# Feed-forward product from split operands: the low parts are formed in the bank by the tensor engine

## What is computed

```python
x = layernorm(x + mixer(x))
h = einsum('bsd,nrd->nbsr', x, lora_A)
coef = (2.0 * lora_weights)[:, None, None]
lora_out = einsum('nbsr,nor->bso', h, lora_B * coef)
base = einsum('bsd,od->bso', x, W) + bias
x = layernorm(x + base + lora_out)
```

## Time and profile before

| | |
|---|---|
| median of 3 runs | 1603.32 us (1602.87 to 1603.79) |
| the profiled execution | 1602.69 us, its span 1600.8 us |
| PE busy | 1579.3 us, 99% of the span |
| DVE busy | 1350.8 us, 84% |
| POOL busy | 1229.3 us, 77% |
| ACT busy | 1223.6 us, 76% |
| mean granted clock of PE | 0.999 of full speed |
| PE's share of the chain that ended last | 95% |

### The profile page before, as it was taken

One profiled execution on the slowest core, in us unless ns is written; L12 is line 12 of the kernel. 1 busy time (PEld: TensorE's weight loads), 2 busy tenths in 40 slices (PEclk: granted clock), 3 DMA queues, 4 the chain that ended last, 5 costly groups with the idle time before them and its releaser, 6 DMA issues.

```text
span 1600.8 us, 27372 instructions
## 1 busy us (share of the span) xinstructions
PE 1579.3 (99%) x9112; PEld 1300.4 (81%) x9112; DVE 1350.8 (84%) x1878; ACT 1223.6 (76%) x2367; POOL 1229.3 (77%) x1019
## 2 busy tenths in 40 slices
PE   8999999999999999999999999999999999999998
PEld 6778888888888888888888888888888888888765
DVE  6776898879979798787988879887998879888797
ACT  5888778886778877887877877888777886778743
POOL 4578788787796868778787887878688786887874
PEclk9999999999999999999999999999999999999999
DMA  3732324233242433433243332433324333343311
GB/s 116 251 129 90 123 81 158 82 116 107 90 143 94 123 99 100 129 100 119 81 123 128 99 122 74 146 102 108 115 87 139 103 116 105 101 129 99 124 55 60
DMA packets 87148, 178.69 MB, mean 112 GB/s; under 512 B 16480, under 2 KB 20576, under 8 KB 86624
## 3 DMA queue, kind: packets, MB, share of 16 engines
q1 hardware_dynamic: 86000, 176.77, 34.1%
q10 hardware_dynamic: 1008, 0.17, 0.1%
HBM read 172.17 MB, written 4.72 MB: 111 GB/s over the span
## 4 chain that ended last, share of the span: by engine, by line
PE 95%; POOL 1%; DVE 1%; issue 1%; DMA 1%; ACT 1%; ACTq 0%; POOLq 0%; SPq 0%; DVEq 0%
PE proj L513 16%; PE proj L514 16%; PE proj L515 16%; PE p_yd L689 8%; PE p_out L561 7%; PE p_out L563 7%; PE p_out L562 7%; PE p_st L570 5%; PE p_hid L525 4%; PE proj L625 2%; PE p_st L699 1%; PE p_st L701 1%; PE p_st L700 1%; PE p_misc L536 1%; DMA raw<-w_t 0%
## 5 line engine op out<-in xcount | busy, mean ns | idle before, releaser
L513 PE MATMUL proj<-x_hi,w_hi 128*128 128x512 f32 x1160 | 461.8, 398 | 8.2 <-DVE x_lo L1300 6.9
L514 PE MATMUL proj<-x_lo,w_hi 128*128 128x512 f32 x1160 | 452.9, 390 | 0.0
L515 PE MATMUL proj<-x_hi,w_lo 128*128 128x512 f32 x1160 | 452.9, 390 | 0.0
L1018 POOL TENSOR_TENSOR w_lo<-raw,w_hi 128x512 fp32r<-128x512 f32 x209 | 284.2, 1364 | 103.7 <-ACT w_hi L751 100.8
L1175 DVE SCALAR_TENSOR_TENSOR hs<-proj,uch,hs 128x511 f32<-128x511 f32 (+2 forms) x384 | 285.6, 744 | 42.8 <-ACT hs L778 38.0
L832 ACT ACTIVATE decay<-decay,tok 128x128 f32<-128x128 f32 x1024 | 312.4, 391 | 0.0
L513 PEld LDWEIGHTS proj<-x_hi,w_hi 128*128 128x128 f32 x1160 | 218.8, 189 | 54.1 <-issue 12.0
L515 PEld LDWEIGHTS proj<-x_hi,w_lo 128*128 128x128 f32 x1160 | 218.3, 188 | 45.9
L514 PEld LDWEIGHTS proj<-x_lo,w_hi 128*128 128x128 f32 x1160 | 218.9, 189 | 42.2
L1204 DVE TENSOR_TENSOR decay<-decay,cb 128x1024 f32<-128x1024 f32 x128 | 200.0, 1563 | 54.7 <-ACT decay L850 53.0
L1076 POOL TENSOR_TENSOR dh<-dh,eac 128x512 f32<-128x512 f32 x96 | 127.2, 1325 | 144.5 <-DVE eac L1235 144.5
(11 more groups left out here) (138 smaller groups left out, 3029.1 us busy)
## 6 DMA issues: line engine op xcount, KB each, us to landing
decay<-acum_d SPq DMA_DIRECT2D x128, 512.0 KB, 4.4
raw<-w_t SPq DMA_DIRECT2D x209, 256.0 KB, 3.0
eac<-eacum_d SPq DMA_DIRECT2D x192, 128.0 KB, 3.0
wo_raw<-wo_t SPq DMA_DIRECT2D x32, 256.0 KB, 4.0
c_new<-wo_t SPq DMA_DIRECT2D x32, 256.0 KB, 4.3
hs<-x_t SPq DMA_DIRECT2D x8, 256.0 KB, 5.6
acc<-x_tok SPq DMA_DIRECT2D x1, 2048.0 KB, 8.2
out<-acc SPq DMA_DIRECT2D x8, 256.0 KB, 2.0
```

The costliest lines, as they stand in the source:

```text
L513: nc.tensor.matmul(dst[:], w_hi[:, ws, k, :], x_hi[:, k, cols], start=(k == 0), stop=False)
L514: nc.tensor.matmul(dst[:], w_hi[:, ws, k, :], x_lo[:, k, cols], start=False, stop=False)
L515: mm = nc.tensor.matmul(dst[:], w_lo[:, ws, k, :], x_hi[:, k, cols], start=False, stop=(k == KC - 1))
L1018: nc.gpsimd.tensor_tensor(w_lo[:, s].rearrange("p a b -> p (a b)"), raw[:, s, :], w_hi[:, s].rearrange("p a b -> p (a b)").bitcast(F32), A ...
```

## The change

The weight and the turned tile are split into high and low fp32r parts, and the product of a tile becomes twelve fp32r products instead of four fp32 ones. The low part is made in the bank: ACT copies the bank rounded into the high part, PE adds minus that high part through a negative identity (fold_rest for the weight, the first product of ffn for the tile), and ACT copies what is left as the low part. PE also adds the weight itself to the low-rank product by an identity in fp32, and DVE's fold_weight goes. The split weight lies in x_hi and x_lo, the split tile in w_hi and w_lo, which the mixer no longer needs then. The negative identity is written by ACT into x_hi.

In order: fold_rest(0) ends step 2 on PE; fold_rest(1) and turn(0) stand in step 3 before and after project_out(2), fold_rest(2) ends it; fold_rest(3) and project_out(3) stand ahead of ffn(0) in step 4. ACT's folded_lo(1) opens step 3 and folded_lo(3) step 4, ahead of gaps and exponentials; turned_lo(c - 4) stands behind them. In the tail ffn(4) comes ahead of turn(5), ffn(5) and ffn(6) have a turn between their high and their low products, and the last tile is done whole. DVE adds it and takes its statistics whole.

```diff
+        yT_hi, yT_lo = lambda t: w_hi[:, t % 2], lambda t: w_lo[:, t % 2]
+        ffn_w_hi, ffn_w_lo = lambda k: x_hi[:, k, 0:HID], lambda k: x_lo[:, k, 0:HID]
+        minus_ident = x_hi[:, 0, HID:HID + P]
...
                 wait(pe, w_folded, k - 1)
                 nc.tensor.matmul(FFN_BANK(k), lora_a_sb[:, k * P:(k + 1) * P], lora_b_sb, start=True, stop=False)
+                nc.tensor.matmul(FFN_BANK(k), ident[:], ffn_w_sb[:, k, :], start=False, stop=False)
...
+            def fold_rest(k):
+
+                pe.wait_ge(fold_hi_ready, k + 1)
+                nc.tensor.matmul(FFN_BANK(k), minus_ident, ffn_w_hi(k), start=False, stop=True,
+                                 skip_group_check=True).then_inc(fold_rest_ready, 1)
...
             def ffn(t, between=None):
 
+                pe.wait_ge(yt_hi_ready, t + 1)
+                nc.tensor.matmul(proj[0][:], minus_ident, yT_hi(t).rearrange("p k l -> p (k l)"), start=False, stop=True,
+                                 skip_group_check=True).then_inc(yt_rest_ready, 1)
                 pe.wait_ge(w_folded, KC)
                 wait(pe, ffn_sum, t - 1)
-                pe.wait_ge(yt_copied, t + 1)
                 for k in range(KC):
-                    if k == 2 and between is not None:
-                        turn(between)
-                    mm = nc.tensor.matmul(FFN_BANK(t), yT(t)[:, k, :], ffn_w_sb[:, k, :], start=(k == 0), stop=(k == KC - 1))
+                    nc.tensor.matmul(FFN_BANK(t), yT_hi(t)[:, k, :], ffn_w_hi(k), start=(k == 0), stop=False)
+                    nc.tensor.matmul(FFN_BANK(t), yT_hi(t)[:, k, :], ffn_w_lo(k), start=False, stop=False)
+                if between is not None:
+                    turn(between)
+                pe.wait_ge(yt_lo_ready, t + 1)
+                for k in range(KC):
+                    mm = nc.tensor.matmul(FFN_BANK(t), yT_lo(t)[:, k, :], ffn_w_hi(k), start=False, stop=(k == KC - 1))
                 mm.then_inc(ffn_out, 1)
...
+                        if ffn_step and c in (3, 4):
+                            fold_rest(2 * c - 5)
+                        if ffn_step and c == 4:
+                            project_out(g, e, 3)
                         if ffn_step and c >= 4:
                             ffn(c - 4)
                         if ffn_step and c in (4, 5, 6):
                             carried_out(g, e, c + 1)
-                        if ffn_step and c >= 3:
+                        if ffn_step and c >= 4:
                             turn(c - 3)
...
                             fold_lora(0)
                             fold_lora(1)
+                            fold_rest(0)
                         if ffn_step and c == 3:
+                            turn(0)
                             fold_lora(2)
                             fold_lora(3)
+                            fold_rest(2)
 
             groups(body)
+            ffn(4)
             turn(5)
-            ffn(4)
             project_out(G, 1, 7)
             norm_sum(G, 7, True)
-            turn(6)
-            ffn(5)
+            ffn(5, between=6)
             ffn(6, between=7)
-            last_ffn()
+            ffn(7)
...
+            def turned_hi(t):
+
                 act.wait_ge(ln_turned, t + 1)
                 wait(act, ffn_out, t - 1)
-                nc.scalar.activation(yT(t), proj[0][:].rearrange("p (k l) -> p k l", k=KC),
-                                     ACT.Copy).then_inc(yt_copied, 1)
+                nc.scalar.activation(yT_hi(t), proj[0][:].rearrange("p (k l) -> p k l", k=KC), ACT.Copy).then_inc(yt_hi_ready, 1)
+
+            def turned_lo(t):
+
+                act.wait_ge(yt_rest_ready, t + 1)
+                nc.scalar.activation(yT_lo(t), proj[0][:].rearrange("p (k l) -> p k l", k=KC), ACT.Copy).then_inc(yt_lo_ready, 1)
...
+                        if last and e == 1 and c in (3, 4):
+                            folded_lo(2 * c - 5)
                         o2, e2, c2 = ahead(e, c, 2)
...
+                        if last and e == 1 and c >= 4:
+                            turned_lo(c - 4)
                         late = c == 1 or (last and e == 1)
                         act.wait_ge(gated, s + 1)
...
                         if last and e == 1 and c >= 3:
-                            copy_turned(c - 3)
+                            turned_hi(c - 3)
...
+                            if c in (2, 3):
+                                folded_hi(2 * c - 4)
+                                folded_hi(2 * c - 3)
+                                folded_lo(2 * c - 4)
...
+                            nc.scalar.activation(minus_ident, ident[:], ACT.Copy, scale=-1.0).then_inc(coef_ready, 1)
 
             groups(body)
-            copy_turned(5)
+            turned_lo(4)
+            turned_hi(5)
             centre(6)
+            turned_lo(5)
             normalize(3)
-            copy_turned(6)
+            turned_hi(6)
+            centre(7)
+            turned_lo(6)
             normalize(4)
-            centre(7)
-            copy_turned(7)
+            turned_hi(7)
+            turned_lo(7)
             normalize(5)
             normalize(6)
...
-            def fold_weight(k):
-
-                dve.wait_ge(lora_ready, k + 1)
-                nc.vector.tensor_tensor(ffn_w_sb[:, k, :], ffn_w_sb[:, k, :], FFN_BANK(k), ALU.add).then_inc(w_folded, 1)
...
-            for t in range(5, CHUNKS - 1):
+            for t in range(5, CHUNKS):
                 add_ffn(t)
                 ln_begin(1, t)
```

More of the change, by code:

```diff
@@ L200, in mixer_ffn_kernel @@
         ffn_loaded, coef_ready, stored = sem("ffn_loaded"), sem("coef_ready"), sem("stored")
-        lora_ready, w_folded = sem("lora_ready"), sem("w_folded")
-        ln_turned, yt_copied, ffn_out, ffn_sum = sem("ln_turned"), sem("yt_copied"), sem("ffn_out"), sem("ffn_sum")
+        lora_ready, fold_hi_ready, fold_rest_ready, w_folded = (
+            sem("lora_ready"), sem("fold_hi_ready"), sem("fold_rest_ready"), sem("w_folded"))
+        ln_turned, yt_hi_ready, yt_rest_ready, yt_lo_ready, ffn_out, ffn_sum = (
+            sem("ln_turned"), sem("yt_hi_ready"), sem("yt_rest_ready"), sem("yt_lo_ready"), sem("ffn_out"), sem("ffn_sum"))
         sc = [hs[:, 1, k, :] for k in range(UT)] + [half[:, 2 * k:2 * k + 2, :].rearrange("p a b -> p (a b)") for k in range(4)]
@@ L609, in turn @@
             def turn(t):
                 pe.wait_ge(centred, t + 1)
-                wait(pe, yt_copied, t)
+                wait(pe, yt_lo_ready, t)
                 for k in range(KC):
-                    mm = nc.tensor.transpose(proj[0][:, k * P:(k + 1) * P], acc[:, t, k * P:(k + 1) * P], ident[:])
+                    mm = nc.tensor.matmul(proj[0][:, k * P:(k + 1) * P], acc[:, t, k * P:(k + 1) * P], ident[:], start=(k == 0), stop=(k == KC - 1),
+                                          is_transpose=True)
@@ L626, in ffn @@
-                mm.then_inc(ffn_out, 1)
[L630 to L638, removed]
+                    nc.tensor.matmul(FFN_BANK(t), yT_hi(t)[:, k, :], ffn_w_hi(k), start=(k == 0), stop=False)
@@ L714, in body @@
                                 carried_out(g, e, 2)
-                        if c:
+                        if ffn_step and c == 4:
+                            pass
+                        elif c:
                             project_out(g, e, c - 1)
@@ L818, in normalize, with folded_hi, folded_lo @@
                                      bias=shift[:, t:t + 1]).then_inc(normed, 1)
-            def copy_turned(t):
+            def turned_hi(t):
                 act.wait_ge(ln_turned, t + 1)
                 wait(act, ffn_out, t - 1)
-                nc.scalar.activation(yT(t), proj[0][:].rearrange("p (k l) -> p k l", k=KC),
-                                     ACT.Copy).then_inc(yt_copied, 1)
+                nc.scalar.activation(yT_hi(t), proj[0][:].rearrange("p (k l) -> p k l", k=KC), ACT.Copy).then_inc(yt_hi_ready, 1)
+            def turned_lo(t):
+                act.wait_ge(yt_rest_ready, t + 1)
+                nc.scalar.activation(yT_lo(t), proj[0][:].rearrange("p (k l) -> p k l", k=KC), ACT.Copy).then_inc(yt_lo_ready, 1)
+            def folded_hi(k):
+                act.wait_ge(lora_ready, k + 1)
+                nc.scalar.activation(ffn_w_hi(k), FFN_BANK(k), ACT.Copy).then_inc(fold_hi_ready, 1)
+            def folded_lo(k):
+                act.wait_ge(fold_rest_ready, k + 1)
+                nc.scalar.activation(ffn_w_lo(k), FFN_BANK(k), ACT.Copy).then_inc(w_folded, 1)
             def gaps(g, e, c):
@@ L1433, in body @@
                             scale_off(g, e, c + 1)
-                        if ffn_step and c == 3:
-                            fold_weight(2)
-                            fold_weight(3)
                         if ffn_step:
                             low_gated(s)
-                        if ffn_step and c == 2:
-                            fold_weight(0)
-                            fold_weight(1)
             groups(body)
```

17 lines of the change are left out of this document (1 added, 16 removed).

## The result

The changed kernel takes 1606.13 us (median of 21 runs, 1603.43 to 1608.19) where the kernel before takes 1603.43 us beside it (1602.20 to 1604.82). The ratio is 1.0016, 95% interval 1.0011 to 1.0022, which is 2.7 us slower (1.8 to 3.5). That is within the 0.2% (3.2 us) that I called "the same", though the interval reaches just over it. It is on the side of the forecast, 1.1 us more than the +1.6 us that I had added up: 1606.13 us where I had 1604.9.

The account below looks back on a forecast made before the run. PE and DVE were near their limit, with ACT and POOL releasing them. Product's end 0.0, unsplit tail 0.5 and one clock fall 1.1 sum to +1.6 us: 1604.9 us beside the median, range 1600.0 to 1608.0.

Parts of the forecast that it names:

- the fall at 1538: PE's clock at half speed in ffn(0) of the kernel before, a loss of 1.97 us, should go with the pauses filled.
- The pause in ffn(0): PE, done with its high products at 1543.0, waits 0.8 us for ACT's turned_lo(0).
- that in ffn(2): In step 6 PE waits about 3.6 us for ACT's turned_lo(2), with a fall of the clock expected behind it.
- case 1: The forecast: DVE and ACT set the pace and the clock falls once, 1604.9 us; chance 0.40.
- case 2: DVE and ACT set the pace without a fall of the clock, 1603.8 us; chance 0.22.
- case 5: The clock falls after each of PE's new pauses; two falls at full price, +4.4 us, 1607.7 us; chance 0.20.
- Case 4: PE alone sets the pace and the copies slip in unseen, -5.1 us, 1598.2 us; chance 0.13.
- the size of the fall: Behind PE's pause in ffn(2), carried_out(7) delayed by up to 1.97 us, of which 1.1 us reach y(7).
- The pause of 1.5 us that I predicted in ffn(4): PE, through its high products at 1579.6, waits 1.5 us for turned_lo(4), which stands behind normalize(2) on ACT.
- step 4: ACT's folded_lo(3) waits for fold_rest(3), delaying exponentials; DVE's scaling of eac comes 1.7 us late, y(5) 0.9 us.
- the unsplit tail: The last addition and its statistics, no longer split in halves, cost 0.5 us more on the last chain.
- PE prices: On PE, a token tile's feed-forward product takes 2.96 us for 3.43, gaining 0.47; the last tile gains nothing.

Follow-up runs that it names:

- three_blocks: The kernel before with the fold on PE and ACT, product unsplit, and the fourth feed-forward block of tiles 0 to 3 left out: 1601.71 us, ratio 0.9989.
- hi_thrice: The changed kernel with the eight high products of tile 2 made three times, each time afresh: 1605.48 us, ratio 1.0013.
- three_moves: The changed kernel with ACT's folded_lo(3) put between two exponentials, turned_lo(2) at the head of step 6, turned_lo(4) ahead of centre(5): 1602.63 us, ratio 0.9993.
- carried_ahead: three_moves with carried_out(5) placed between project_out(3) and ffn(0) on PE: 1600.84 us, ratio 0.9984.
- lora_twice: The kernel before with the low-rank product of each of the four blocks made twice, DVE adding as before: 1603.40 us, ratio 1.0001.
- fold_only_ffn4: The kernel before with the fold on PE and ACT, product unsplit, and ffn(4) ahead of turn(5) in the tail: 1600.64 us, ratio 0.9984.
- tail_halves: The changed kernel with the last tile's product, addition and statistics in two halves again: 1606.01 us, ratio 1.0016.
- fold3_later: The changed kernel with ACT's folded_lo(3) between two exponentials instead of ahead of the gaps: 1605.54 us, ratio 1.0010.
- lo2_ahead: The changed kernel with ACT's turned_lo(2) opening step 6, ahead of gaps and exponential of chunk 7: 1604.51 us, ratio 1.0008.

## Why the prediction was right, and where it was off

All times here are in the frame of before (after less 2.10 us).

**Right.** The fp32r products follow each other in 0.22 to 0.23 us (1551.20 and 1551.42). PE's pauses up to 1540 are filled and the fall at 1538 is gone. mix(5) starts at 1542.4 (predicted 1542.3), eac(5) at 1546.0 (1545.9), y(5) at 1550.6 (1550.4). The pause in ffn(0) is 0.78 us (0.8), that in ffn(2) 3.55 (3.6), turned_lo(2) starts at 1564.0 and ends 0.58 later, at 1564.6 (1564.4). One fall of the clock follows. So it is case 1: case 2 (no fall) is against the mean clocks of all runs, and case 5 (falls behind the other pauses too) against the trace, in which the clock stays full behind the 0.78 us, though the one fall lasts as long as the two of case 5 would. Case 4, that PE alone sets the pace, falls with three_blocks: in steps 5 and 6 it does not.

**Off: the size of the fall, and half a microsecond without it.** I let 1.1 us of the fall reach y(7), by DVE's slack, and from there the end. y(7) is at 1574.56, where I had 1573.1 + 1.1 = 1574.2, a little more. But the fall lasted 6.8 us, twice the one that I had priced. (That price, 1.97 us, was itself a little high: it compares a record, 5.40 us, with a distance of starts, 3.43; carried_out(5) starts at 1543.06, 5.23 us behind the start of the product, so the loss was 1.80.) The longer fall cost PE 2.9 us: 1.87 for the four low products that take 0.91 at full clock, and 6.43 us from carried_out(7) to the product into p_yd (1568.60 to 1575.03), where the kernel before takes 4.53:

```profile
1563.40 1.05 PE L570 MATMUL p_st<-cT,state 128*128 128x128 f32 x8
...
1567.93 1.09 PE L689 MATMUL p_yd<-decay,xdt 128*64 128x128 f32 x16
...
1592.01 1.89 PE L637 MATMUL proj<-hs,raw 128*128 128x256 f32 x8
```

PE, which I held to be ahead, was thereby the path itself: it was busy for 32.20 of the 32.20 us from 1566.80 to 1599.00. The pause of 1.5 us that I predicted in ffn(4) shrank to 0.14, because PE came late itself. The last tile starts 2.5 us later than before (1594.49 for 1592.01), where my terms give 1592.6 + 1.1, 1.7 us later. 0.8 us are missing.

hi_thrice divides them. It has the same waits and no fall, and it starts the last tile at 1593.02 (1595.81 less its own offset of 2.79 us; its y(2) is at 1521.36). So the fall is worth 1.47 us there, 0.4 more than my 1.1. The other 0.4 have nothing to do with the clock: without a fall I had 1592.6. Of them 0.27 stand in turned_lo(4), which lets PE go on at 1581.42 where I had 1581.15, and the rest in the work behind it. The mechanism was right; the term for the fall should have been 1.5, and the product's end without a fall was not level with the kernel before but 0.4 us behind it.

**Right in the sum, off in the reason: step 4.** I named ACT's folded_lo(3) as the new wait. It costs 1.0 us. Once it is out of the way, PE's own order costs more: carried_out(5) stands behind both project_out(3) and ffn(0), and with ffn(0) moved behind it 1.74 us come back between three_moves and carried_ahead. That project_out(3) alone, moved back, would give the same was not run. My arithmetic had it in it (it counted the 2.8 us of project_out ahead of ffn(0)), so that eac(5) came out right, but I did not see it as a cause of its own that the moved step puts on DVE.

**Right in the net: the last tile.** +0.5 for the unsplit tail and -0.5 for the shorter product were both in the sum, though my passage on PE prices says that the last tile gains nothing. It does: from its first product to DVE's last addition it takes 3.21 us for 3.66, and from there to the end 5.60 us for 5.13. From the first product of the tile to the last power it is 5.24 us in both kernels.

**Where the gain went.** The fold part alone gives about 2 us. The split product with its order costs 4.5 to 5 on top. By the distances from y(2) to the end, after and carried_ahead differ by 5.63 us: 1.04 is the place of folded_lo(3), 1.74 that of carried_out(5), 1.27 in y(5) to y(7) the place of turned_lo(2) with the fall behind it, and 1.5 that of turned_lo(4). Each of these is a difference of two single profiles; of the runs, the intervals of neighbouring steps overlap, and only the sum is clear of noise. What the split product saves on PE, 0.47 us a tile, comes to nothing in steps 5 and 6: y(5) to y(7) is 22.65 to 22.97 us in all kernels without a fall there, except lora_twice with 23.15. Only behind y(7), where PE sets the end, may it show: 26.9 us with the split product, 27.5 with fold_only_ffn4, two kernels that differ in more than the product. And it is lost again ahead of y(5) (29.26 for 28.80), so that the two are level from y(2) to the end, 79.10 and 78.99 us.

## What to carry to other kernels

A step moved ahead on one engine delays everything that stood between its old and its new place; ask of each instruction there who waits for it. Where two or three engines are near their limit, a cheaper product on one of them is worth nothing until its copies on the others stand where nobody waits for them; here the places decided 5.6 us, and even with all of them well placed the split product was only level with the unsplit one. Price a possible fall of the clock on the engine's own path and as if it may last twice as long as the one you have seen.

## What the runs showed of the hardware that I had not expected

- After much the same pause of PE (2.3 to 2.6 us, near 80 us) the clock fell in twelve profiles and not in two, and a fall was 3.4 or 6.8 us long, with nothing in the kernel to tell them apart. Behind the pause of 3.55 us it fell in the profiles of after and tail_halves for 6.8 us and in that of fold3_later for 3.4. Behind single pauses of 0.98, 1.41 and 1.65 us (lo2_ahead) it stayed full. What decides isn't settled.
- In the runs of the changed kernel the time goes with the mean granted clock: medians of 1607.5 us at 0.995, 1606.6 at 0.996, 1605.2 at 0.997 and 1604.0 at 0.998. Such falls can be most of the 4.8 us between its fastest and its slowest run. They are not the whole of it: the runs of hi_thrice, all at 0.998 or 0.999, still spread over 3.5 us.
- A half-width fp32r product (256 columns) follows the last in 0.12 us, about half of the 0.227 of the full one, so that no fixed cost per product is seen at that width (tail_halves).
- The products into a bank that holds transposes, with the negative identity, need no time beyond their own: 0.23 us (1541.37 to 1541.60 in three_moves).
